# Cross-attention on one core: PV for two tiles of keys at a time, three buffers of exponentials, and inverses spread in the transpose

## The reference

```python
qn = _layer_norm(Q, ln_q_g, ln_q_b)
q = (qn @ Wq + bq)                         # heads of 16
k, v = (KV @ Wk + bk), (KV @ Wv + bv)
attn = softmax(q @ k.T / sqrt(16))         # per head, 512 x 1601
x = Q + (concat_heads(attn @ v) @ Wo + bo)
h = _layer_norm(x, ln_ff_g, ln_ff_b)
out = x + silu(h @ W1 + b1) @ W2 + b2
```

## Time and profile before

| | |
|---|---|
| median of three runs | 3684.07 us |
| the profiled execution | 3687.68 us |
| its span | 3685.9 us, mean granted clock 0.988 |
| TensorE matmul busy | 3508.9 us |
| VectorE busy | 2494.4 us |
| ScalarE busy | 2244.5 us |
| GpSimd busy | 929.4 us |

### The profile page before, as it was taken

How to read it: one execution, slowest core, us unless ns; L and a number is a source line. 1 busy time by engine, 2 the same in 40 slices (tenths; PEclk the granted TensorE clock), 3 DMA queues, 4 the chain that set the end, 5 groups by cost and what they waited for, 6 DMA issues and landing times.

```text
span 3685.9 us, 52544 instructions
## 1 busy us (share of the span) xinstructions
PE 3508.9 (95%) x19620; PEld 1556.0 (42%) x19620; DVE 2494.4 (68%) x4643; ACT 2244.5 (61%) x2979; POOL 929.4 (25%) x1341
## 2 busy tenths in 40 slices
PE   5899999999999999999999999999999999999997
PEld 2333443444434444444444434444444444434435
DVE  5777767676676766767676676766767676676761
ACT  1466666656666566666656666566666656666564
POOL 1122314222231212313222231222313223132202
PEclk7999999999999999999999999999999999999998
DMA  4222212232121321212222122321213222122200
GB/s 95 60 40 39 49 30 53 42 65 40 25 52 35 66 42 33 51 32 58 42 59 38 28 52 39 66 39 35 46 33 63 42 42 50 30 52 42 42 7 12
DMA packets 121535, 162.96 MB, mean 44 GB/s; under 512 B 37040, under 2 KB 102592, under 8 KB 118208
## 3 DMA queue, kind: packets, MB, share of 16 engines
q1 hardware_dynamic: 120896, 159.40, 22.1%
q10 hardware_dynamic: 384, 0.20, 0.0%
HBM read 46.43 MB, written 8.39 MB: 15 GB/s over the span
## 4 chain that ended last, share of the span: by engine, by line
PE 80%; DVE 14%; ACT 3%; issue 2%; SPq 1%; DMA 0%; POOL 0%; ACTq 0%; DVEq 0%
PE o_ps L1171 20%; PE rows_ps L1137 19%; PE scores L1152 14%; DVE chunk_max L955 9%; PE side L1111 6%; PE side L1114 6%; PE side L1100 5%; PE side L1092 5%; PE side L1096 2%; PE side L1104 1%; ACT probs L803 1%; DVE stats L834 1%; DVE resid L861 1%; PE side L1107 0%; PE side L1086 0%
## 5 line engine op out<-in xcount | busy, mean ns | idle before, releaser
L955 DVE TENSOR_REDUCE chunk_max<-rows_ps 128x1 f32<-128x512 f32 (+1 forms) x3328 | 2111.3, 665 | 1052.7 <-PE rows_ps L1137 1044.3
L803 ACT ACTIVATE probs<-scores 128x1024 f32<-128x1024 f32 (+1 forms) x1664 | 1677.0, 1024 | 1136.7 <-PE scores L1152 1129.7
L1137 PE MATMUL rows_ps<-k_stack,q_stack 96*128 96x512 bf16 (+1 forms) x4096 | 1216.2, 339 | 97.1 <-DVE chunk_max L955 55.7
L1152 PE MATMUL scores<-q_stack,k_stack 99*128 99x512 bf16 (+1 forms) x3328 | 1037.2, 380 | 7.2 <-DMA q_stack<-shift_parts 4.2
L1171 PE MATMUL o_ps<-probs,v_sb 128*32 128x512 f32 x6656 | 886.4, 605 | 0.4 <-ACT probs L803 0.4
L1137 PEld LDWEIGHTS rows_ps<-k_stack,q_stack 96*128 96x128 bf16 x4096 | 332.0, 97 | 1191.0 <-DVE chunk_max L955 971.3
L1152 PEld LDWEIGHTS scores<-q_stack,k_stack 99*128 99x128 bf16 (+1 forms) x3328 | 324.8, 100 | 297.2 <-issue 37.3
L573 POOL TENSOR_TENSOR rest<-whole,k_parts 128x512 f32<-128x512 f32 x124 | 116.8, 942 | 969.8 <-ACT k_parts L748 965.4
L1111 PE MATMUL side<-hT,w_sb 128*128 128x256 f32 x968 | 259.8, 381 | 0.0
L1171 PEld LDWEIGHTS o_ps<-probs,v_sb 128*32 128x32 f32 x6656 | 130.9, 108 | 294.3 <-issue 220.4
L1100 PE MATMUL side<-wv_sb,ctxT 128*128 128x128 f32 (+1 forms) x1664 | 244.5, 279 | 7.3 <-DMA cf_c<-in_L_xattn_ln_ff_b 2.8
(11 more groups left out here) (107 smaller groups left out, 2049.5 us busy)
## 6 DMA issues: line engine op xcount, KB each, us to landing
k_stack<-k_parts SPq DMA_DIRECT2D x768, 50.0 KB, 2.2
k_stack<-k_stack SPq DMA_DIRECT2D x192, 200.1 KB, 5.6
ctx_nat<-in_ctx SPq DMA_DIRECT2D x47, 512.0 KB, 4.0
q_stack<-q_stack SPq DMA_DIRECT2D x192, 64.0 KB, 3.4
q_stack<-q_parts SPq DMA_DIRECT2D x756, 16.0 KB, 1.8
x_nat<-in_x SPq DMA_DIRECT2D x16, 512.0 KB, 6.1
resid<-in_x SPq DMA_DIRECT2D x32, 256.0 KB, 2.7
out<-resid SPq DMA_DIRECT2D x32, 256.0 KB, 2.5
```

The lines of the kernel that those rows point to most:

```text
L803: nc.scalar.activation(probs[0:rows, (q + t) % 2, 2 * LQ * pair:2 * LQ * (pair + 1)], scores[0:rows, 2 * LQ * pair:2 * LQ * (pair + 1)], A ...
L955: nc.vector.tensor_reduce(dst, src, AX.X, ALU.max).then_inc(rows_read, 1)
L1137: last = nc.tensor.matmul(rows_ps[:, m % 2, d0:d0 + w], q_stack[s][0:STACK, h, P * t:P * (t + 1)], k_stack[s][0:STACK, h, k0:k0 + w], star ...
L1152: ins = nc.tensor.matmul(scores[0:keys_in(t), LQ * j:LQ * (j + 1)], k_stack[s][:, h, P * t:P * t + keys_in(t)], q_stack[s][:, h, :], start ...
```

## The change

PV is no longer placed in every tile. In each even tile from 2 on TensorE gets the PVs of the two tiles before it (t - 2 and t - 1) as two pieces of the plan; in tile 0 the PV of tile 12 of the quarter before; in odd tiles none. `probs` gets a third buffer, and buffers are counted through over quarters and batches. The exponential of tile t now waits for the PV of tile t - 3. In the inversion the copy into `spread` is left out: the transpose back reads the reciprocals through a view that repeats each 16 times, with a column of zeros beside it.

```diff
+BUFFERS = 3
+def pv_tiles(t):
+    return [KT - 1] if t == 0 else [t - 2, t - 1] if t % 2 == 0 else []
+def probs_buffer(b, q, t):
+    return ((b * 4 + q) * KT + t) % BUFFERS
...
@@ plan
-            work += [(u, "pv", None)] * (u % 2)
+            work += [(u, "pv", i) for i in pv_tiles(t)] * (u % 2)
...
-DVE_SEQ_PER_BATCH = 58
+DVE_SEQ_PER_BATCH = 54
...
-        probs = sb("probs", [P, 2, 4 * LQ])
+        probs = sb("probs", [P, BUFFERS, 4 * LQ])
-        inverse = sb("inverse", [P, LQ // 32])
-        spread = sb("spread", [P, LQ // 32, 3 * DH])
+        inverse = sb("inverse", [P, LQ // 32, 3])
...
@@ scalar, quarter
-                        wait(act, pv_done, per_quarter(KT, b, q, t - 1))
-                    nc.scalar.activation(probs[0:rows, (q + t) % 2, 2 * LQ * pair:2 * LQ * (pair + 1)],
+                        wait(act, pv_done, per_quarter(KT, b, q, t + 1 - BUFFERS))
+                    nc.scalar.activation(probs[0:rows, probs_buffer(b, q, t), 2 * LQ * pair:2 * LQ * (pair + 1)],
...
@@ vector, invert_denominators
-                    link(nc.vector.reciprocal(inverse[:, :], blocks[:, :, DH - q % 2]))
-                    link(nc.vector.tensor_copy(spread[:, :, DH:2 * DH],
-                                               inverse[:, :].unsqueeze(2).broadcast_to((P, LQ // 32, DH))))
-                    first = DH * (1 - q % 2)
-                    nc.vector.transpose(blocks, spread[:, :, first:first + 32]).then_inc(inverted, 1)
+                    link(nc.vector.reciprocal(inverse[:, :, 1], blocks[:, :, DH - q % 2]))
+                    first = 1 - q % 2
+                    nc.vector.transpose(denom[:, :].rearrange("p (c e r) -> p c e r", e=2, r=DH),
+                                        inverse[:, :, first:first + 2].unsqueeze(3).broadcast_to((P, LQ // 32, 2, DH)))\
+                        .then_inc(inverted, 1)
...
@@ tensor, quarter
                         elif u > 1:
-                            multiply_v(b, q, u // 2 - 1)
+                            multiply_v(b, q, arg)
                         elif q > 0:
-                            multiply_v(b, q - 1, KT - 1)
-                        elif not (isinstance(b, int) and b == 0):
-                            multiply_v(b - 1, 3, KT - 1)
+                            multiply_v(b, q - 1, arg)
+                        elif b > 0:
+                            multiply_v(b - 1, 3, arg)
```

More of the change, by code:

```diff
@@ L971, in prologue @@
             def prologue():
-                nc.vector.memset(spread[:, :, :], 0.0)
+                nc.vector.memset(inverse[:, :, :], 0.0)
                 for stage in range(STAGES):
@@ L1171, in multiply_v @@
                     last = nc.tensor.matmul(o_ps[32 * j:32 * j + 32, :], v_sb[q // 2][0:rows, t, col:col + 32],
-                                            probs[0:rows, (q + t) % 2, LQ * j:LQ * (j + 1)],
+                                            probs[0:rows, probs_buffer(b, q, t), LQ * j:LQ * (j + 1)],
                                             start=(t == 0), stop=(t == KT - 1))
```

## The result

The changed kernel takes 3789.52 us (median of four runs, 3788.14 to 3791.05) against 3684.00 us for the kernel before (four runs here): 1.0285 times as long, 95% interval 1.0273 to 1.0298. The profiled executions took 3790.56 and 3687.68 us. The prediction was 3773 us, range 3722 to 3805.

What follows compares the result with a forecast made beforehand. TensorE's instruction stream was taken as the bound. Terms of 5.9 us a batch times 14 gave 82, plus 2.5 for batch 0 and 4 for the last: 89 us more, so 3773 us, range 3722 to 3805.

Steps and rivals of the forecast that it cites:

- k to k, twice: Odd to even tile, quarters 1 and 3: second k product waits 0.92 us for ScalarE's copies to free the side bank.
- w1 to w1: Quarter 2, tiles 9-10: next w1 product waits 1.25 us for ScalarE's copies out of the side bank.
- score on the exponential of tile 5, quarter 2: Tile 6's third score product waits for tile 5's second exponential, TensorE arriving 1.09 earlier: +1.1 us a batch.
- quarter 0, tiles 4 to 8, behind wo: TensorE waits in tile 5 for VectorE's sum, statistics and reads, partly regained in the tiles behind: +1.0 us a batch.
- switches saved, two pairs: Only two pairs a batch come out adjacent, each saving TensorE a 0.18 us switch of shape: -0.36 us a batch.
- inversion: One 0.29 us copy leaves VectorE, which binds in tile 1 of quarter 1: -0.3 us a batch.
- relief of the maxima: Light tiles: new order ends tiles in a single M, relieving 1.0 of 6.1 us a batch of late M's.
- Adjacent pairs: Rival (a): pairs adjacent after all, 384 switches gone and waits hidden, 3615 us; chance 1%.
- Relief of the maxima: Rival (b): single M's between PVs feed VectorE evenly, all 17 late M's (6.1 us a batch) go: 3671 us; chance 10%.
- Slow transpose of a repeated view: Rival (c): the inversion's broadcast transpose takes 0.6 us more in tile 1, 64 times: 3811 us; chance 7%.
- Half of the waits: Rival (d): about half the waits come, as ScalarE and VectorE run earlier in even tiles: 3727 us; chance 12%.
- The rule that was weighed: Weight loads overlap matmuls only in differing row groups; then adjacent pairs save nothing and the sum is 94, not 89 us.

Runs made afterwards that it cites:

- the copy put back: Changed kernel plus a VectorE copy of 256 repeated reciprocals between reciprocal and transpose, standing in for the spread copy: 3786.71 us, 1.0291 of before.
- with three buffers: Changed kernel with the PV of tile t - 1 again in every tile, so three buffers and new inversion but no pairs: 3683.10 us, 0.9999 of before.
- the maxima placed otherwise: Changed kernel, pairs kept, with the planner's PV cost 1024 instead of 2048 and maxima phase 0.35 instead of 0.5: 3726.40 us, 1.0117 of before.
- the new placing: Kernel before with new inversion, one PV a tile, planner's PV cost 1024 instead of 2048, maxima phase 0.35 instead of 0.5: 3604.13 us, 0.9786 of before.

## Why the prediction was right, and where it was off

**Right: which way and why.** The planner puts a maximum between the PVs, 37 of the 384 pairs of the launch come out adjacent (28 of them in batches 1 to 14, two a batch, as counted ahead), and each odd tile uncovers waits that PV had covered. Term by term, a steady batch, start to start (wait after, less what stood there before):

| step of the prediction | forecast | measured |
|---|---|---|
| k to k, twice | 1.84 | 1.94 |
| w1 to w1 | 1.25 | 1.37 |
| w1 to k | 0.73 | 0.84 |
| v to v, twice | 0.82 | 1.04 |
| x to x | 0.8 | 0.75 |
| score on the exponential of tile 5, quarter 2 | 1.1 | 1.11 |
| quarter 0, tiles 4 to 8, behind wo | 1.0 | 0.70 |
| switches saved, two pairs | -0.36 | -0.46 |
| inversion (from the copy put back) | -0.3 | -0.36 |
| relief of the maxima (not measured: what is left) | -1.0 | -0.87 |
| sum | 5.9 | 6.06 |

The last term is what makes the sum come out. A check from another side: over the whole batch the time lost ahead of M's falls by 0.7 (8.0 to 7.3), although the place behind wo adds to it and the inversion takes 0.3 off.

The exponential's row, to lay beside the earlier trace rows (timeline, TensorE and ScalarE, quarter 2, tiles 5 and 6 of the changed kernel):

```profile
1375.65 0.81 PE L1165 MATMUL scores<-q_stack,k_stack 99*128 99x512 bf16 x3
...
1376.85 2.98 ACT L816 ACTIVATE probs<-scores 128x1024 f32<-128x1024 f32 x3
...
1377.95 0.39 PE L1165 MATMUL scores<-q_stack,k_stack 99*128 99x512 bf16 x1 [1.49 <-ACT probs L816]
```

And VectorE behind wo, beside the earlier trace rows (TensorE and VectorE, quarter 0, tile 5):

```profile
1263.09 0.68 DVE L874 TENSOR_TENSOR resid<-side,resid 128x512 f32<-128x512 f32 x1
...
1263.45 0.38 PE L1165 MATMUL scores<-q_stack,k_stack 99*128 99x512 bf16 x1
...
1265.20 0.39 PE L1150 MATMUL rows_ps<-k_stack,q_stack 96*128 96x512 bf16 x1 [1.37 <-DVE chunk_max L968]
...
1265.21 0.66 DVE L968 TENSOR_REDUCE chunk_max<-rows_ps 128x1 f32<-128x512 f32 x1
...
1266.27 1.88 DVE L968 TENSOR_REDUCE chunk_max<-rows_ps 128x1 f32<-128x512 f32 x3
```

TensorE has a score at 1263.45 and its next product, an M, at 1265.20: 1.53 of waiting in one place, while VectorE works through the sum and the statistics. Tile 5 took 3.88, put at 4.1.

**A little off: each restart of the side bank.** Four of the five side terms came out 0.05 to 0.12 per place too low. The step that was short is "the bank is free 1.52 + 0.06 after k's end: wait 0.92": the restarted product itself takes 0.96 instead of 0.86, because its first weight load waited with it and is no longer hidden (the rows of tile 8 above). The switch was sized at 0.18 and is 0.23, because the third and fourth wave follow closer than the second follows the first; on two pairs a batch that is nothing.

**Off by a term that is missing: the clock.** The sum was 89 us for the launch, measured are 103 between the profiled executions: 85 from the steady batches (forecast 82), 2.7 and 4.9 from the first and the last (2.5 and 4), 13.1 from eight falls of the clock, and 2.8 less before the first score. The prediction spoke of the granted clock only as 1.00 in the kernel before and took it over, so these 13 us stood at nothing. The 4.9 of the last batch are loose: the kernel before took 250.0 us in it, but with the inversion alone, or with three buffers, it took 247.2 and 246.2, with the clock falling at its end each time, by differing amounts. That the falls come with the pairs around tiles 5 and 11 of quarter 0 is shown by taking just these two pairs away. It is not the pairs as such: with the maxima placed otherwise the same pairs stand there, TensorE is busy 2.43 of 2.79 us in tile 5 and 2.32 of 2.79 us in tile 11, and no batch before the last has a fall. The rest of the distance between forecast and median is that the profiled run of before was 3.7 us above its median, and that of the change only 1.0.

**The rivals.** *Adjacent pairs* (3615): the order was not adjacent, and made so it is 3871: the waits are not hidden, and this is the worst case and not the best. *Relief of the maxima* (3671): the 6.1 us a batch that it rests on are real, as the new placing makes likely, which takes 5.0 a batch back, but pairs are no means to it. *Slow transpose of a repeated view* (3811): no, the 64 transposes take 711 ns, against 712 in the earlier trace rows:

```profile
L954 DVE STREAM_TRANSPOSE denom<-inverse 128x512 f32<-128x512 f32 x64 | 45.5, 711 | 2.2
```

*Half of the waits* (3727): no, they all came, and only the one behind wo clearly smaller (0.70 for 1.0).

**The rule that was weighed.** The sentence of the Trainium skill's "TensorE: Matmul & The Clock Gate" (Part 3, The mechanism) by which loads for the same row group would not be hidden would have an adjacent pair save nothing; it saves 0.23. For this shape (32 columns, f32) the measurement decides against the sentence. The prediction left out that the same section also lets a load run ahead when it goes to the background weight buffer; with that the measurement agrees, and so read the section never stood against the forecast.

## What to carry to other kernels

Before work is lumped to save a fixed cost, ask what it covers where it is taken away: here 0.23 us a pair stood against 0.4 to 1.4 us in each place where a buffer between engines was then emptied in the open. Read the order that the planner makes, not the one that the change is named for; and try the planner's own constants first, since two numbers were worth 2.1% here. A new idle stretch on TensorE can cost a second time, by the clock: here 13 us of 103.

## What the runs showed of the hardware

Eight PV instructions on four groups of 32 columns take 1.00 us to the next product, sixteen 1.85, and the entrance from a full-width product some 0.09 in both cases. A restart after a wait for the side bank makes the two f32 instructions of k 0.10 longer (0.96 against 0.86); a bf16 product for scores that waited for the exponential took 0.22 to the next start, as without a wait (1377.95 to 1378.17). In the changed kernel TensorE's granted clock fell to its lower level for 3.4 us only behind tiles in which TensorE was busy 2.5 or 2.75 of 3.9 us, but not each time: nine of the 14 steady batches kept it up with the same tiles in them. Between the four runs of the kernel with pairs and a copy put back, the whole time differed by 21 us and the mean clock with it (0.983 in the slowest, 0.988 to 0.989 in the others). What decides whether it falls was not tried.
